# Softmax row totals in groups of four key tiles: one product with ones per group, three adds on GpSimd and VectorE

## What is computed

```python
def _L0_attn_ref(x, w_attn, w_proj, adapter_wte, gating):      # x: 1 x 2048 x 1024, 32 heads of 32
    q, k, v = split(x @ w_attn.T); q, k = rope(q), rope(k)
    scores = q @ k.T / sqrt(32), causal
    y = softmax(scores) @ v
    y = y + gating * softmax(q @ ak.T / sqrt(1024)) @ av        # ak, av: keys and values of 10 adapter rows
    return y @ w_proj.T
h = layernorm(x) * (1 + ca) + sa;  x = x + ga * attention(h)
h = layernorm(x) * (1 + cb) + sb;  x = x + gb * top2_of_8_experts(h)
```

## Time and profile before

| | |
|---|---|
| median of 3 runs | 2745.73 us (2738.48 to 2749.93) |
| the profiled execution | 2743.38 us, of it span 2741.5 us |
| attention steps | 875.8 to 1968.1 us: 1092.3 us |
| TensorE busy in them | 1072.67 us |
| VectorE, ScalarE, GpSimd busy in them | 774.24, 642.13, 774.81 us |
| products with ones (line 1103) | 154.6 us busy, x1296 |
| GpSimd's adds (line 1306) | 687.8 us busy, x321 |

### The profile page before, as it was taken

One profiled execution on the slowest core, in us unless ns is written; L12 is line 12 of the kernel. 1 busy time (PEld: TensorE's weight loads), 2 busy tenths in 40 slices (PEclk: granted clock), 3 DMA queues, 4 the chain that ended last, 5 costly groups with the idle time before them and its releaser, 6 DMA issues. The chain is left out here.

```text
span 2741.5 us, 40031 instructions
## 1 busy us (share of the span) xinstructions
PE 2482.9 (91%) x13407; PEld 1621.5 (59%) x13407; DVE 1624.8 (59%) x3253; ACT 1056.7 (39%) x1885; POOL 1320.2 (48%) x827
## 2 busy tenths in 40 slices
PE   6789999998758999999999999999779875999997
PEld 4667677777534444444444444444258764888885
DVE  5544555110458777777777777777136554767666
ACT  3521001111331555555555555555411111444443
POOL 3452442000432767676767676667624453333332
PEclk8999999999886999999999999999989987999998
DMA  7356655312743515151515151511186755878875
GB/s 263 108 155 198 176 168 170 95 39 61 262 134 80 133 39 133 37 134 37 135 37 136 36 134 38 121 47 48 31 274 215 168 117 179 304 280 302 296 283 195
DMA packets 231902, 397.20 MB, mean 145 GB/s; under 512 B 44540, under 2 KB 95292, under 8 KB 231620
## 3 DMA queue, kind: packets, MB, share of 16 engines
q1 hardware_dynamic: 204340, 319.62, 40.2%
q0 software_dynamic: 17152, 50.38, 5.3%
q10 hardware_dynamic: 10256, 25.21, 2.9%
HBM read 299.22 MB, written 103.76 MB: 147 GB/s over the span
## 5 line engine op out<-in xcount | busy, mean ns | idle before, releaser
L1184 ACT ACTIVATE t_prob<-t_scores_psum 128x512 f32<-128x512 f32 (+3 forms) x1280 | 610.5, 538 | 440.0 <-PE t_scores_psum L1076 241.8
L1306 POOL TENSOR_TENSOR t_two<-t_prob 128x1024 f32<-128x1024 f32 (+1 forms) x321 | 687.8, 2165 | 164.7 <-ACT t_prob L1184 110.9
L1212 DVE TENSOR_REDUCE t_part<-t_seen_psum 128x1 f32<-128x512 f32 x768 | 479.2, 682 | 141.0 <-PE t_seen_psum L1049 137.0
L1049 PE MATMUL t_seen_psum<-t_k_stack,t_q_stack 97*128 97x512 f32 (+3 forms) x1283 | 522.0, 419 | 39.6 <-DVE t_q_stack L1200 22.5
L1072 PE MATMUL t_scores_psum<-t_q_stack,t_k_stack 98*128 98x512 f32 (+3 forms) x1280 | 502.8, 404 | 5.3 <-ACT t_prob L1184 3.9
L1072 PEld LDWEIGHTS t_scores_psum<-t_q_stack,t_k_stack 98*128 98x128 f32 x1280 | 241.9, 190 | 301.5 <-ACT t_prob L1184 165.5
L1049 PEld LDWEIGHTS t_seen_psum<-t_k_stack,t_q_stack 97*128 97x128 f32 x1283 | 256.8, 201 | 90.8 <-DVE t_part L1212 36.8
L1218 DVE CUSTOM_DVE_ANT_0 t_seen_psum<-t_seen_psum,t_causal 128x128 f32<-128x128 f32 (+3 forms) x515 | 250.6, 504 | 100.9 <-PE t_seen_psum L1049 89.8
L1090 PE MATMUL t_y_acc_psum<-t_prob,t_v 128*32 128x512 f32 (+3 forms) x2576 | 301.4, 540 | 0.0
L1591 PE MATMUL z_acc_psum<-z_e_hi,z_x_hi 128*128 128x512 f32 x576 | 228.1, 396 | 0.0
L1593 PE MATMUL z_acc_psum<-z_e_hi,z_x_lo 128*128 128x512 f32 x576 | 224.9, 390 | 0.0
(11 more groups left out here) (234 smaller groups left out, 3892.7 us busy)
## 6 DMA issues: line engine op xcount, KB each, us to landing
z_raw<-in_expert_w SPq DMA_DIRECT2D x80, 512.0 KB, 6.8
z_spare<-in_expert_w SPq DMA_DIRECT2D x72, 512.0 KB, 7.1
f_w_raw<-in_wmod SPq DMA_DIRECT2D x8, 2048.0 KB, 10.1
t_q_stack<-scratch_q_hi SPq DMA_DIRECT2D x64, 256.0 KB, 5.1
t_k_stack<-scratch_k_hi SPq DMA_DIRECT2D x64, 256.0 KB, 5.0
f_w_raw<-in_w_attn SPq DMA_DIRECT2D x24, 512.0 KB, 7.0
t_inverse<-scratch_inverse SPq DMA_DIRECT2D x132, 64.0 KB, 2.0
t_y<-scratch_a_y SPq DMA_DIRECT2D x33, 256.0 KB, 4.5
```

What stands on the lines that cost most here:

```text
L1049: nc.tensor.matmul(seen[:, n % BANKS, 0:width], q_stack[par][0:SEEN, h, t0:t0 + P], k_stack[par][0:SEEN, h, c * CH:c * CH + width], start= ...
L1184: nc.scalar.activation(prob[:, step % RING, h, c0:CH], scores[:, score_bank(step, h), c0:CH], ACT.Exp, scale=1.0 / math.sqrt(D)).then_inc( ...
L1212: nc.vector.tensor_reduce(dst, seen[:, n % BANKS], AX.X, ALU.max).then_inc(seen_free, 1)
L1306: nc.gpsimd.tensor_tensor(two[:, pair % 2, heads, c0:CH], a, b, ALU.add).then_inc(two_ready, 1)
```

## The change

Four steps, not two, share one product with ones. GpSimd adds steps 0 and 1 of a quad into `two` (two instructions of two heads), then step 2 (two more); VectorE adds step 3 by one instruction of all four heads, behind slot 1 of the step after the quad. `add_up` runs behind steps 3, 7, 11, ... for the quad before, always in all 512 columns.

```diff
-    PAIRS = STEPS // 2
+    QUADS = STEPS // 4
+    ADDS = 4
...
-            def add_up(i, pair):
+            def add_up(i, quad):
-                wi, kt = steps[2 * pair]
-                c0 = first_column(2 * pair)
-                pe.wait_ge(two_ready, (i * PAIRS + pair) * 2 + 6)
+                wi, kt = steps[4 * quad]
+                n = i * QUADS + quad
+                pe.wait_ge(two_ready, (n + 2) * ADDS)
+                pe.wait_ge(third_ready, n + 2)
...
                 for h in range(HG):
-                    last = nc.tensor.matmul(total[h * D:(h + 1) * D, c0:CH], ones[:, :], two[:, pair % 2, h, c0:CH],
-                                            start=(kt == 0), stop=(kt == steps_of(UNITS[wi][1]) - 2))
+                    last = nc.tensor.matmul(total[h * D:(h + 1) * D, :], ones[:, :], two[:, quad % 2, h, :],
+                                            start=(kt == 0), stop=(kt == steps_of(UNITS[wi][1]) - 4))
...
-                if step % 2 == 1:
-                    add_up(i, (step - TOTAL_LAG - 1) // 2)
+                if step % 4 == TOTAL_LAG - 1:
+                    add_up(i, (step - TOTAL_LAG) // 4)
...
-                    if step % 2 == 0:
-                        act.wait_ge(two_ready, (i * PAIRS + step // 2) * 2 + 2)
+                    if step % 4 != 1:
+                        act.wait_ge(two_ready, (i * QUADS + step // 4) * ADDS + {0: 2, 2: 4, 3: 4}[step % 4])
+                    if step % 4 == 3:
+                        act.wait_ge(third_ready, i * QUADS + step // 4 + 1)
...
+            def add_third(i, quad):
+                n = i * QUADS + quad
+                c0 = first_column(4 * quad + 3)
+                dve.wait_ge(two_ready, (n + 1) * ADDS + 4)
+                dve.wait_ge(exp_done, (i * STEPS + 4 * quad + 3) * HG + HG + BANKS)
+                at = two[:, quad % 2, 0:HG, c0:CH]
+                nc.vector.tensor_tensor(at, at, prob[:, (4 * quad + 3) % RING, 0:HG, c0:CH], ALU.add).then_inc(third_ready, 1)
...
             def finish(i, step):
+                if step % 4 == 0 and 0 < i * STEPS + step <= STEPS * (G // 2):
+                    add_third(i, step // 4 - 1)
...
                 if half == 0:
-                    pool.wait_ge(exp_done, (i * STEPS + 2 * pair + 1) * HG + HG + BANKS)
-                    pool.wait_ge(total_done, i * PAIRS + pair + 1)
+                    pool.wait_ge(exp_done, (i * STEPS + 4 * quad + 1) * HG + HG + BANKS)
+                    pool.wait_ge(total_done, n)
...
+            def add_more(i, quad, x, half):
+                n = i * QUADS + quad
+                c0 = first_column(4 * quad + x)
+                heads = slice(half * HALF, (half + 1) * HALF)
+                pool.wait_ge(exp_done, (i * STEPS + 4 * quad + x) * HG + (half + 1) * HALF + BANKS)
+                pool.wait_ge(two_ready, (n + 1) * ADDS + 2 * (x - 1) + half)
+                at = two[:, quad % 2, heads, c0:CH]
+                nc.gpsimd.tensor_tensor(at, at, prob[:, (4 * quad + x) % RING, heads, c0:CH], ALU.add).then_inc(two_ready, 1)
...
             def finish(i, step):
-                if step % 2 == 0:
-                    add_two(i, step // 2 - 1, 1)
+                if step % 4 == 2:
+                    add_two(i, step // 4, 1)
+                if step % 4 == 3:
+                    add_more(i, step // 4, 2, 0)
+                    add_more(i, step // 4, 2, 1)
                 for wi in ended(i, step, SPLIT_LAG):
                     split(i, wi)
```

More of the change, by code:

```diff
@@ L865, in attention @@
         scores_ready, exp_done, sums_set, cleared = sm("scores_ready"), sm("exp_done"), sm("sums_set"), sm("cleared")
-        y_done, two_ready, total_done, y_free, total_free = sm("y_done"), sm("two_ready"), sm("total_done"), sm("y_free"), sm("total_free")
+        y_done, two_ready, third_ready, total_done, y_free, total_free = sm("y_done"), sm("two_ready"), sm("third_ready"), sm("total_done"), sm("y_free"), sm("total_free")
         tall_loaded, inverted, inverse_kept, inverse_loaded = sm("tall_loaded"), sm("inverted"), sm("inverse_kept"), sm("inverse_loaded")
@@ L1165, in take_total @@
             def take_total(i, wi):
-                act.wait_ge(total_done, i * PAIRS + last_step(wi) // 2 + 3)
+                act.wait_ge(total_done, i * QUADS + (last_step(wi) + 1) // 4 + 1)
                 act.wait_ge(tall_loaded, (i * W + wi + 2) * 16)
@@ L1195, in _ @@
             dve.sem_inc(tall_loaded, 16)
+            dve.sem_inc(third_ready, 1)
             dve.sem_inc(y_done, RING - Y_LAG)
@@ L1283, in _ @@
             pool.sem_inc(y_lo_done, 1)
-            pool.sem_inc(two_ready, 3)
+            pool.sem_inc(two_ready, ADDS)
             for b in range(2):
@@ L1290, in _, with add_two @@
             pool.wait_ge(sums_set, 2)
-            def add_two(i, pair, half):
-                c0 = first_column(2 * pair)
+            def add_two(i, quad, half):
+                n = i * QUADS + quad
+                c1 = first_column(4 * quad + 1)
                 heads = slice(half * HALF, (half + 1) * HALF)
                 if half == 0:
-                    pool.wait_ge(exp_done, (i * STEPS + 2 * pair + 1) * HG + HG + BANKS)
-                    pool.wait_ge(total_done, i * PAIRS + pair + 1)
-                    c1 = first_column(2 * pair + 1)
-                    if c1 > c0:
+                    pool.wait_ge(exp_done, (i * STEPS + 4 * quad + 1) * HG + HG + BANKS)
+                    pool.wait_ge(total_done, n)
+                    if c1 > 0:
                         pool.sem_inc(marks, 1)
-                        nc.gpsimd.memset(prob[:, (2 * pair + 1) % RING, :, c0:c1], 0.0).then_inc(cleared, 1)
-                        pool.wait_ge(cleared, (i * W + steps[2 * pair][0]) * (TPC // 2) + (c0 > 0) + 1)
-                a, b = (prob[:, (2 * pair + x) % RING, heads, c0:CH] for x in range(2))
-                nc.gpsimd.tensor_tensor(two[:, pair % 2, heads, c0:CH], a, b, ALU.add).then_inc(two_ready, 1)
+                        nc.gpsimd.memset(prob[:, (4 * quad + 1) % RING, :, 0:c1], 0.0).then_inc(cleared, 1)
+                        pool.wait_ge(cleared, i * W + steps[4 * quad][0] + 1)
+                a, b = (prob[:, (4 * quad + x) % RING, heads, :] for x in range(2))
+                nc.gpsimd.tensor_tensor(two[:, quad % 2, heads, :], a, b, ALU.add).then_inc(two_ready, 1)
+            def add_more(i, quad, x, half):
+                n = i * QUADS + quad
+                c0 = first_column(4 * quad + x)
[4 more added lines that the diff above has]
+                nc.gpsimd.tensor_tensor(at, at, prob[:, (4 * quad + x) % RING, heads, c0:CH], ALU.add).then_inc(two_ready, 1)
             def split(i, wi):
@@ L1324, in _ @@
                     finish(i, step)
-                    if step % 2 == 1:
-                        add_two(i, step // 2, 0)
+                    if step % 4 == 1:
+                        add_two(i, step // 4, 0)
             for step in range(SPLIT_LAG + 1):
-                if step == 0:
-                    add_two(G // 2, -1, 1)
                 for wi in ended(G // 2, step, SPLIT_LAG):
```

## The result

| | before | after |
|---|---|---|
| median | 2743.69 us (4 runs) | 2913.6 us (4 runs, 2905.71 to 2928.09) |
| ratio | | 1.0619, 95% interval 1.0595 to 1.0644 |
| up to the first exponential | 875.9 us | 881.3 us |
| attention, first to last exponential | 1092.2 us | 1274.1 us |
| tail | 773.5 us | 770.9 us |

The change costs 170 us where 100 were forecast, and lies above the range. The last three rows are of the two profiled executions. The one after is the longest of its four (2928.09 us), so the stages differ by 185 in sum: +182 in the attention, +5 ahead of it, -3 in the tail.

What follows compares the result with a forecast made beforehand. TensorE's order was taken to bound the attention, with VectorE next. From 2743.4 us, 55 saved on products with ones, 71 added for VectorE's adds, 71 and 13 for held divisions gave 2843 us (+3.6%); range 2765 to 2890.

Steps and rivals of the forecast that it cites:

- Bound and direction: In the attention steps: TensorE's order bounds, VectorE is next in line; the change makes the kernel slower, +3.6%.
- GpSimd's run of 9.7 us: After a full quad's second step: GpSimd's four adds run in a row, taking 9.7 us with lags.
- X4: Start of the first score in the step after a full quad, where VectorE's add stands behind slot 1.
- The add of 2.27 us: VectorE's new 2048-element add after a full quad: 2.27 us, by the slope of shorter adds; its stops cost 71 us.
- The division held 5.3 us: At unit ends: the division meets GpSimd's adds and holds VectorE 5.3 us; +71 us at full quads, 13 at diagonal.
- The stops: 155 us forecast: TensorE waiting for banks in the attention: 71 us from adds, 71 and 13 from divisions, at an unchanged clock.
- The 55 us saved: TensorE's products with ones in the attention: 122.9 us before, 68.0 after, so 55 us less.
- rival 3: GpSimd and VectorE hold each other up further (split meets add, late exponentials): 2890 us and more; chance 0.1.
- rival 1: Division held once or briefly, costing TensorE 0 to 40 us: 2760 to 2800 us; chance 0.2.
- Rivals 2 and 4: Add short enough for the banks, 2688 to 2715 us, chance 0.1; stalls cancel the saving, 2735 to 2758, chance 0.05.
- the 1.25 of the banks: Between VectorE's maxima of slots 1 and 2: an add up to 1.25 us would not stop TensorE.
- What would show it: Trace signs: 48 adds of about 2.3 us, `see` waits some 150 us, divisions averaging 1.5 us up, TensorE 85 to 90% busy.

Runs made afterwards that it cites:

- late_divide: Changed kernel, VectorE's add kept, with the division and split one step later; 2925.6 us, ratio 1.0640.
- no_third: Changed kernel without VectorE's add of the fourth step, so totals are wrong; attention 1134.6 us, whole 2821.5 us.
- no_third_spread: Changed kernel without VectorE's add (totals wrong), division and split in the last slot of the step after the quad, store and adapter load later; attention 1072.3 us.
- later_add: Changed kernel with VectorE's whole add moved one step later, behind GpSimd's run; 2821.1 us, ratio 1.0268.
- spread: Changed kernel with VectorE's add one step later, division and split in the last slot of the step after the quad, store and adapter load later; 2837.2 us, ratio 1.0317.
- diag_quads: Change applied only to each unit's last four (diagonal) steps, full ones kept in pairs as in the kernel before; 2777.5 us, ratio 1.0124.
- warm: Changed kernel plus useless 512-column TensorE products where it was seen to stop; 2926.3 us, ratio 1.0652.

## Why the prediction was too small

**Bound and direction: right.** TensorE's order bounds the stage, VectorE is next in line, and a VectorE that frees no bank stops TensorE. The rows show it as drawn, with `see` the product that waits.

**GpSimd's run of 9.7 us: right in length, in the wrong place.** In the quad shown it lasts from 1955.00 to 1964.78. The forecast had it end at X4 + 2.4; X4 is 1961.03 here, so it ends at X4 + 3.8. There ScalarE copies `y` out (0.60 us from 1953.84, after a wait of 1.21) ahead of the last exponential, and the run starts some 1.8 us later than I had it; I had taken the start from a later step of a unit. In a unit's third quad it ends at X4 + 0.8 to 1.6, and the add does not wait. In sum the 45 long adds wait 19.0 us, which happens to be what 0.4 us each would give (18). The short adds, which I had wait for nothing, wait 10.6 us behind the eight quads that are a unit's only one; idle time there rose by 5.4.

**The add of 2.27 us: right.** 31 of the 48 lasted 2274 to 2293 ns; the other 17, up to 2669, met GpSimd. The 2.19 us that I had estimated from the table in the Trainium skill, VectorE: DVE Perf Modes, is too low here. The same section says under the table that its row under-predicts, and gives 2291 ns for such an add of 2048 elements, with which these rows agree; I had overlooked that.

**The division held 5.3 us: found, but oversized.** The mean is 3.88 us, and only 6 of 33 are over 4.5. And its 71 us were no term of their own: late_divide made it free and the time stayed. The forecast added the two stops where they share one burst on VectorE: behind the 23 full quads with a division it had 104.6 us, and idle time rose there by 45.5.

**The stops: 155 us forecast, 91 measured**, as TensorE's idle time. This is where the sum was too high, by 64 us, of which 59 are those 23 places. The 15 first quads without a division were right (28.5 and 29.8).

**The 55 us saved: too high.** With half level priced at one half, the busy time is lower by 46 us in the changed kernel, 48 in no_third and 46 in no_third_spread, but only 24 in later_add. As stage time no_third_spread gives 20, because its idle time grows by 18 and half level costs 9. No run gave the 55.

**The step that failed: "TensorE stops", priced at the length of the stop and no more.** The sum had no term for the granted clock, and took 1.00 from the earlier trace rows as if it belonged to the stage and not to TensorE's work without stops. It was 279.9 us at half level against 6.8 before, 137 us of time. An error of the other sign, 64 us of idle time too many, hid part of it; the saving, 9 us too large, went the same way as the missing term: 100 - 64 + 9 + 137 = 182.

**Rivals.** The time fell where rival 3 had it (2890 and more), and its mechanism is there in part: split and add meet (L1340 has a mean of 1584 ns, 1280 alone), and late exponentials delay GpSimd. That its time fell out is in large part luck, as it had no clock in it either. For rival 1, which had the division cost 0 to 40 us, speaks that without the add the division's stops are small: no_third idles 18 us more than no_third_spread. Against it, those stops took 92 us at half level with them. Rivals 2 and 4 are out: 2.28 us is well over the 1.25 of the banks, though behind a third quad that add stopped TensorE for only 0.4 us.

**What would show it** held for the adds, the division's means (1.59 and 2.17 us), and front and tail (+5 and -3). `see` waits were forecast at some 150 us rather than 35, the sum of two rows; the same two rows have 87.4 + 60.6 = 148, and with the masked maxima it is 230 against 42. TensorE's busy share is 91%, not 85 to 90: a share can look healthy because the engine works at half level. The clock beside it says so.

**Open.** Why idle plus half of half level less 46 underestimates spread, later_add and diag_quads (there less 14) by 15 to 22 us; why some stops bring a fall of the clock and others of the same length do not; how a dip's length is set; and how much of no_third_spread's missing saving is VectorE's load at a unit's start and how much `invert` waiting for its transfer. None of these was tried apart. Nor was the division ever further from the add than in later_add.

## What to carry to other kernels

An item taken from the engine that bounds and given to another pays only if that other has room at that very place: ask how long it will not serve its oldest duty, whatever fills that time, before counting its busy share. Price every new stop of TensorE with the half-level stretch that may follow it, keep two stops from falling together, and read the granted clock beside the busy share. Ahead of adding a VectorE instruction with two SBUF inputs, lay GpSimd's runs beside it; cutting it into pieces gives GpSimd more chances to hold it, and moving it past the run is worth more than halving it.

## What the runs showed of the hardware

- In the changed kernel all 36 stops of TensorE of 1.3 to 3.0 us were followed by a fall to the 1.2 GHz level; its 46 slow stretches were 6.1 us long on average. Idle time added up to 111 us and slow stretches to 280. In later_add 66 stops of 0.6 to 1.3 us were followed by ten such falls, and 80 us of idle time by 89 us at half level.
- Some 144 us of products of no use, put where the stops were, left the stage within 4 us of its length (warm).
- A 1024-element add of VectorE that began 0.03 us behind a GpSimd add lasted 3.40 instead of some 1.2 us.
